# A perceiver layer on one core: the fourth piece of the scan moved around chunk 0's first products, the squares' tiles moved, and VectorE's first chunk reordered

## What is computed

```python
x = x + xattn(layernorm(x), ctx_1024, ...)     # attention over 257 context rows
h = layernorm(x)
xg = h * sigmoid(h @ Wg.T + bg)                # the gated tokens
# a linear scan over the 32 tokens, for each channel with its own 16x16 matrix A:
s = s @ A + xt * Bp;  y = (s * Cp).sum() + Dp * xt
y = y + xg
x = x + layernorm(y) * gamma + beta
h = layernorm(x) @ ternary(w_fc).T + gate * (layernorm(x) @ v.T @ fast_b.T @ u.T)
r = maximum(h, 0)
x = x + (r * r) @ ternary(w_proj).T
```

## Time and profile before

| | |
|---|---|
| time, median of 3 runs | 505.27 us (503.5 to 507.44) |
| time of the profiled execution | 506.74 us |
| its span on the core | 504.9 us |
| mean granted clock of PE | 0.988 |
| busy: PE, DVE, ACT, POOL | 94%, 81%, 71%, 68% of the span |

### The profile page before, as it was taken

The page is one execution under the profiler, slowest core; times in us unless marked ns, Lnnn a source line. Parts: engine busy times, 40 slices in busy tenths (PEclk is TensorE's granted clock), DMA queues, the critical chain, the costliest instruction groups (busy, mean ns, idle before and its releaser), DMA issues.

```text
span 504.9 us, 13692 instructions
## 1 busy us (share of the span) xinstructions
PE 472.9 (94%) x4374; PEld 403.6 (80%) x4374; DVE 408.9 (81%) x1203; ACT 356.6 (71%) x881; POOL 341.3 (68%) x446
## 2 busy tenths in 40 slices
PE   3799999999999998999999899887999999999995
PEld 2488788788888887888878788675888888888885
DVE  1689988889998899899998977787778798798654
ACT  3767677787877877577778577654877876877752
POOL 1478988776766767567767567222878887887563
PEclk9999999999999999899999899998999999999999
DMA  7944377586655747357657458675103303301102
GB/s 220 309 168 143 131 225 187 158 239 154 212 160 158 215 133 230 119 153 189 194 138 218 138 115 206 129 221 172 30 1 84 86 0 84 85 1 43 43 0 84
DMA packets 77974, 70.40 MB, mean 139 GB/s; under 512 B 40000, under 2 KB 60752, under 8 KB 77392
## 3 DMA queue, kind: packets, MB, share of 16 engines
q1 hardware_dynamic: 77904, 69.54, 48.5%
HBM read 56.87 MB, written 12.65 MB: 138 GB/s over the span
## 4 chain that ended last, share of the span: by engine, by line
PE 58%; DVE 10%; issue 9%; POOL 6%; ACT 3%; SPq 2%; DMA 1%; POOLq 0%; DVEq 0%; ACTq 0%
PE qv_ps L810 16%; PE turn_ps L799 9%; PE att_ps L861 5%; PE gate_ps L889 5%; PE fc_ps L1705 5%; PE score_ps L874 4%; PE proj_ps L1726 4%; POOL sq_lo L1842 3%; PE gate_ps L881 2%; PE feat_ps L850 2%; DVE bn_x L356 1%; PE xt_ps L1697 1%; PE xt_ps L1688 1%; PE feat_ps L930 1%; DVE scan_x L1887 1%
## 5 line engine op out<-in xcount | busy, mean ns | idle before, releaser
L1842 POOL TENSOR_TENSOR sq_lo<-scan_x,sq_hi 128x512 fp32r<-128x512 f32 x63 | 82.9, 1318 | 34.4 <-ACT sq_hi L1797 34.2
L1025 ACT COPY ctxT<-turn_ps 128x512 f32<-128x512 f32 x128 | 68.9, 590 | 33.4 <-PE turn_ps L799 32.0
L1789 ACT ACTIVATE relu<-fc_ps,fc_square 128x512 f32<-128x512 f32 x64 | 43.8, 685 | 33.3 <-PE fc_ps L1711 33.2
L1887 DVE SCALAR_TENSOR_TENSOR scan_x<-fc_ps,relu 128x512 f32<-128x512 f32 x64 | 43.7, 685 | 26.4 <-ACT relu L1789 25.8
L1212 POOL TENSOR_TENSOR hb_lo<-hbT,hb_hi 128x256 fp32r<-128x256 f32 x32 | 25.4, 795 | 49.0 <-ACT hb_hi L1100 49.0
L1705 PE MATMUL fc_ps<-xn_hi,fc_T 128*128 128x512 f32 x128 | 52.1, 407 | 2.1 <-DVE scan_x L1887 2.1
L799 PE MATMUL turn_ps<-ident,ctxn 128*128 128x128 f32 x352 | 49.1, 286 | 3.9 <-ACT ctxT L1025 2.6
L1705 PE MATMUL fc_ps<-xn_lo,fc_T 128*128 128x512 f32 x128 | 50.7, 396 | 0.0
L1204 POOL TENSOR_TENSOR proj_in<-proj_in,below 128x512 f32<-128x512 f32 x31 | 48.1, 1550 | 2.0 <-DVE below L1380 1.8
L1198 POOL TENSOR_TENSOR rstd<-ve,neg_half 128x1 f32<-128x1 f32 x64 | 35.2, 549 | 20.5 <-DVE ve L1445 15.7
L799 PEld LDWEIGHTS turn_ps<-ident,ctxn 128*128 128x128 f32 x352 | 42.4, 148 | 4.8 <-ACT ctxT L1025 3.1
(11 more groups left out here) (250 smaller groups left out, 1455.2 us busy)
## 6 DMA issues: line engine op xcount, KB each, us to landing
ctxn<-in_ctx SPq DMA_DIRECT2D x22, 1024.0 KB, 5.5
toeplitz<-in_ctx SPq DMA_DIRECT2D x10, 1024.0 KB, 5.7
resid<-in_x SPq DMA_DIRECT2D x32, 128.0 KB, 5.5
ctx_end<-in_ctx SPq DMA_DIRECT2D x32, 128.0 KB
gated_tokens<-gated SPq DMA_DIRECT2D x32, 128.0 KB, 6.0
scan_x<-gated_tokens SPq DMA_DIRECT2D x60, 64.0 KB, 4.8
out<-resid SPq DMA_DIRECT2D x7, 512.0 KB, 3.3
scan_quarters<-scan_x SPq DMA_DIRECT2D x3, 1024.0 KB, 5.3
```

Source lines behind the costliest of these rows:

```text
L1025: act.copy(ctxT[:, b, :, 0:J - 1], turn_ps[b % 2][:, :].rearrange("p (k j) -> p k j", k=KD)).then_inc(ctxT_copied, 1)
L1789: act.activation(relu[m % 2], fc_ps[m % 2][:, :], ACT.Relu, scale=fc_square[:, m:m + 1]).then_inc(relu_done, 1)
L1842: pool.tensor_tensor(sq_lo[:, tile(c, m) % PARTS, :], sq[m % SQ], sq_hi[:, tile(c, m) % PARTS, :].bitcast(F32), ALU.subtract).then_inc(sq_ ...
L1887: dve.scalar_tensor_tensor(out=sq[m % SQ], in0=fc_ps[m % 2][:, :], scalar=0.0, in1=relu[m % 2], op0=ALU.max, op1=ALU.mult).then_inc(sq_don ...
```

## The change

Nothing is changed in stage one, on SP or on POOL. In stage three:

- Scan blocks 8 to 11 (third piece) use the banks `proj_ps[0]` and `fc_ps`; blocks 12 to 15 (fourth piece) alternate over the two banks `proj_ps[1]`. `xt_ps` is not used by the scan any more, and `turn_first` has no wait for scan copies.
- PE runs blocks 8 to 13, then `turn_first`, block 14, `low_rank(0)`, both wides and both lows of tiles 0 and 1, block 15, and goes on as before. ACT copies block 14 after the two `xn_hi`, and block 15 in the loop at m = 1, behind `relu_tile(0, 1)` and `square_hi(0, 0)`.
- `sq` lies in `fc_in`, the loaded fc weights, which are turned into `fc_T` by then.
- DVE: the helpers take one half. The order is centre half 0, x of half 0, centre half 1, normalise half 0, x of half 1, `xn_lo` half 0, normalise half 1, y sums of chunk 1 half 0, `xn_lo` half 1, y sums half 1. `second_centre` is split: half 0 where it was, half 1 behind the square of tile 0.

The diff, with the bodies that only moved into helpers of one half cut:

```diff
-            for h in range(2):
-                for r in half(h):
-                    ins = dve.scalar_tensor_tensor(out=y_in[:, r, :], in0=y_in[:, r, :], scalar=mv_y[:, r, 0:1],
...
+        def first_centre(dve, h):
...
+        def first_x(dve, h):
...
+        def first_norm(dve, h):
...
-        def second_centre(dve):
+        def second_centre(dve, h):
...
-            tiles = scan_x[:, :, :].rearrange("p (i t) q -> p i (t q)", i=BATCH * CQ // TOK)
-            sq = [tiles[:, (PIECES - 1) * PB * CQ // TOK + i, :] for i in range(SQ)]
-            assert SQ * TOK <= PB * CQ
+            tiles = fc_in[:, :, :].rearrange("p (i a) d -> p i (a d)", i=SQ)
+            sq = [tiles[:, i, :] for i in range(SQ)]
+            assert SQ * TOK == MT * D
...
-            last_ring = (*proj_ps[0], *fc_ps, *xt_ps)
+            third_banks, fourth_banks = (*proj_ps[0], *fc_ps), proj_ps[1]
+            FOURTH = (PIECES - 1) * BLOCKS
+
+            def scan_bank(n):
+                return third_banks[n % BLOCKS] if n < FOURTH else fourth_banks[n % 2]
+
...
-                    at_least(pe, scan_copied, n - len(last_ring) + 1 if n - len(last_ring) >= 2 * BLOCKS else 0)
-                    scan_products(pe, n, last_ring[n % len(last_ring)])
+                    if n == FOURTH:
+                        pe.wait_ge(w_copied, 11)
+                    at_least(pe, scan_copied, n - 1 if n >= FOURTH + 2 else 0)
+                    scan_products(pe, n, scan_bank(n))
...
                         pe.wait_ge(xn_done, h + 1)
-                        if h == 0:
-                            pe.wait_ge(scan_copied, PIECES * BLOCKS)
...
                     at_least(pe, sq_done, tile(c, m) - 1)
+                    if tile(c, m) < 2:
+                        pe.wait_ge(scan_copied, FOURTH - 1 + m)
...
                         at_least(pe, out_ready, 2 * (c - 1))
+                        if c == 1:
+                            pe.wait_ge(scan_copied, PIECES * BLOCKS)
...
-                for n in range(2 * BLOCKS, PIECES * BLOCKS):
+                for n in range(2 * BLOCKS, FOURTH + 2):
                     last_scan(n)
                 turn_first()
+                last_scan(FOURTH + 2)
                 low_rank(0)
...
                             for i in range(2):
                                 hidden_low(0, i)
+                            last_scan(FOURTH + 3)
...
-                for n in range(2 * BLOCKS, PIECES * BLOCKS):
-                    scan_copy(act, n, last_ring[n % len(last_ring)])
+                for n in range(2 * BLOCKS, FOURTH + 2):
+                    scan_copy(act, n, scan_bank(n))
...
                              ).then_inc(xn_hi_done, 1)
+                scan_copy(act, FOURTH + 2, scan_bank(FOURTH + 2))
                 low_rank_hi(0)
...
                             square_hi(c, m - 1)
+                        if c == 0 and m == 1:
+                            scan_copy(act, FOURTH + 3, scan_bank(FOURTH + 3))
...
-                first_y(dve)
-                first_x(dve)
-                y_sums(dve, 1, range(CH))
-                for h in range(2):
+                def first_lo(h):
...
+                first_y(dve)
+                first_centre(dve, 0)
+                first_x(dve, 0)
+                first_centre(dve, 1)
+                first_norm(dve, 0)
+                first_x(dve, 1)
+                first_lo(0)
+                first_norm(dve, 1)
+                y_sums(dve, 1, half(0))
+                first_lo(1)
+                y_sums(dve, 1, half(1))
                 y_moments(dve, 1)
                 low_rank_parts(0)
-                second_centre(dve)
+                second_centre(dve, 0)
...
                             if m == 0:
+                                second_centre(dve, 1)
                                 second_add(dve, 0)
```

More of the change, by code:

```diff
@@ L259, in first_y @@
                 dve.tensor_scalar(ve_y[:, rows_of(h)], mv_y[:, rows_of(h), 1], EPS, None, ALU.add).then_inc(ve_y_done, 1)
-            for h in range(2):
-                for r in half(h):
-                    ins = dve.scalar_tensor_tensor(out=y_in[:, r, :], in0=y_in[:, r, :], scalar=mv_y[:, r, 0:1],
-                                                   in1=gamma_all[:, :], op0=ALU.subtract, op1=ALU.mult)
-                ins.then_inc(centred, 1)
-        def first_x(dve):
-            for h in range(2):
[L269 to L290, removed]
@@ L292, in second_centre @@
-        def second_centre(dve):
-            dve.wait_ge(mv_y_done, whole_chunks(2))
[L295 to L299, removed]
+        def first_centre(dve, h):
+            for r in half(h):
+                ins = dve.scalar_tensor_tensor(out=y_in[:, r, :], in0=y_in[:, r, :], scalar=mv_y[:, r, 0:1],
+                                               in1=gamma_all[:, :], op0=ALU.subtract, op1=ALU.mult)
+            ins.then_inc(centred, 1)
@@ new lines, in first_x @@
+        def first_x(dve, h):
+            dve.wait_ge(centred, h + 1)
+            dve.wait_ge(rstd_y_done, h + 1)
+            for r in half(h):
+                ins = dve.scalar_tensor_tensor(out=res(0, r), in0=y_in[:, r, :], scalar=rstd_y[:, r:r + 1],
+                                               in1=res(0, r), op0=ALU.mult, op1=ALU.add)
+            ins.then_inc(x2_done, 1)
+            dve.wait_ge(x2_done, h + 1)
+            for r in half(h):
+                ins = dve.bn_stats(bn_x[:, r, :], res(0, r))
+            ins.then_inc(bn_x_done, 1)
+            dve.wait_ge(bn_x_done, h + 1)
+            for r in half(h):
+                ins = dve.bn_aggr(mv_x[:, r, :], bn_x[:, r, :])
+            ins.then_inc(mv_x_done, 1)
+            dve.wait_ge(mv_x_done, h + 1)
+            dve.tensor_scalar(ve_x[:, rows_of(h)], mv_x[:, rows_of(h), 1], EPS, None, ALU.add).then_inc(ve_x_done, 1)
@@ new lines, in first_norm @@
+        def first_norm(dve, h):
+            dve.wait_ge(rstd_x_done, h + 1)
+            for r in half(h):
+                ins = dve.tensor_scalar(xn[:, r, :], res(0, r), mv_x[:, r, 0:1], rstd_x[:, r:r + 1],
+                                        ALU.subtract, ALU.mult)
+            ins.then_inc(xn_done, 1)
+        def second_centre(dve, h):
+            dve.wait_ge(mv_y_done, whole_chunks(2))
+            for r in half(h):
+                ins = dve.scalar_tensor_tensor(out=y_second[:, r, :], in0=y_second[:, r, :], scalar=mv_y[:, r, 0:1],
+                                               in1=gamma_all[:, :], op0=ALU.subtract, op1=ALU.mult)
+            ins.then_inc(centred, 1)
```

## The result

The changed kernel took 512.68 us (median of 4, 510.99 to 515.4) against 506.36 us before (median of 4, 503.5 to 509.28); the ratio is 1.0135 with a 95% interval of 1.0087 to 1.0182: slower by 1.35%, or 6.8 us by the ratio (the two medians lie 6.3 us apart). The forecast was 511.3, range 508.0 to 514.0. Six more executions gave 511.82 against 505.71, ratio 1.0125 (1.0085 to 1.0165). All ratios here leave out four executions that ran in a slower state: two of e3's ten (1162 and 2550 us) and two of the kernel before (511.36 and 512.38 us).

What follows compares the result with a forecast made beforehand. PE was taken to bound the kernel, with chunk 2's delayed load coming onto its path at tile 3. 4.8 + 1.5 - 0.3 = +6.0 us on the median of 505.27 gave 511.3 us, range 508.0 to 514.0.

Steps and rivals of the forecast that it cites:

- The view: PE's waits at the head of stage three decide; what is late at tile 3 is late at the end, us for us.
- Steps 1 and 2: DVE's and PE's head: half 1 normalised 0.9 us later than before, `low_rank(0)` at 342.8 against 342.44.
- step 2: PE's head: half 0 turned at once, half 1 at 340.75 to 341.3, so `low_rank(0)` can start at 342.8.
- Step 3: PE's clock in the head: lows of tiles 0 and 1 0.3 us earlier, bounds -1.2 and +1.0.
- Step 4: Block 15 free in PE's gap, its copy done ten us later; `second_centre` half 1 adds 0.8 us on DVE, hidden.
- Step 5: Chunk 2's load behind the sixteenth copy: 4.5 us from issue to sums, wides of tile 3 +4.8 us.
- Step 6: PE's clock falls after idling before tile 3: slow matmuls cost 1.5 us, bounds 0 and 1.6.
- Step 7: Small waits of PE in chunk 0 are absorbed: -0.3 us, bounds -0.5 and 0.
- the other side: Rival: chunk 2's y is there when DVE asks, blocks 14 and 15 fill gaps, 1.2 us saved, 504.1 us; chance 0.06.
- the cheaper wait: Rival: clock stays up or recovers at once, or the head gains 1.2 us; 4.0 instead of 6.0, 509.3 us; chance 0.08.
- the worse head: Rival: block 14 at half clock delays `low_rank(0)` (+1.0), load takes 5.4 us (+0.9); 513.5 us; chance 0.06.

Runs made afterwards that it cites:

- e3: Changed kernel with the sums of chunk 2's half 0 behind the square of tile 1, load still late; ratio to the kernel before 1.0082.
- a2: The changed kernel measured again, unedited; ratio to the kernel before 1.0125, 182.39 us from the first sums to the end.
- e1: Changed kernel with chunk 2's y loaded ahead of SP's wait for the sixteenth scan copy; ratio to the kernel before 1.0054.
- e5: e1 with `second_centre` whole again, ahead of the square of tile 0; ratio to the kernel before 0.9976.
- e4: Changed kernel with the edits of e1 and e3 together; ratio to the kernel before 1.0061.
- e8: e5 with e3's edit, block 14 ahead of `turn_first` again and DVE's head reordered; ratio to the kernel before 0.9988.
- e6: Kernel before with the sums of chunk 2's half 0 behind the square of tile 1; ratio to the kernel before 0.9984.
- e7: Kernel before with only `second_centre` split, half 1 behind the square of tile 0; ratio to the kernel before 1.0063.
- e2: Kernel before with SP waiting for the high part of tile 0's square before loading chunk 2's y; ratio to the kernel before 1.0112.

## Why the prediction was right, and where it was off

- **The view** held: nothing outside the head of stage three counts, and what is late at tile 3 is late at the end.
- **Steps 1 and 2** (DVE's and PE's head): half 1 was normalised at 10.66 against a forecast of 10.6, and `low_rank(0)` at 13.25, the slow one of the two ends given; block 14 did run at half speed. "The first half is ahead, the second pays for it" is what the trace shows. (The terms of step 2 add up to 342.5 and not to its 342.7; no later step hangs on the difference.) Left open by a2 and the other runs is only which way the clock goes there: e1's `low_rank` stood at 13.65 and its lows at 16.56, e5's at 12.90 and 17.02; in e1 block 14 ran at half pace, in e3, e4 and e5 it did not and the slow matmuls came in `low_rank` instead.
- **Step 3**: the lows at 16.76, forecast 16.4.
- **Step 4**: the sixteenth copy at 19.75 against 19.5; block 15 and its copy cost nothing, as said (e8, e6). What step 4 had wrong is `second_centre` half 1: it was put at 0.8 us, hidden. It was hidden, but it costs 1.9 (e7), since it pushes `second_add` beside POOL. In the changed kernel that made no difference, as DVE was done at 347.99 and waited until 351.04.
- **Step 5**: 4.48 us from issue to sums, forecast 4.5 (a2 4.47, e2 4.09). Tile 3 is +5.00 us, forecast +4.8. This is the mechanism, shown from both sides: e1 takes it out and e2 puts it in.
- **Step 6 failed in size.** The slow matmuls behind the wait were put at 1.5 us, bounds 0 and 1.6, from the 3.4 us that the clock was low in the head of before. After 5.55 us of waiting the matmuls ran at half pace until about 358.4, that is 6.0 us. From the wides of tile 3 to the second projection's start (358.52) it took 6.08 us, before 3.38: 2.70 lost, 2.25 in e2, 1.54 in e7. The upper bound was taken from a single stretch, and it was no bound. The rows of before:

```profile
354.11 0.64 PE L1726 MATMUL proj_ps<-proj_T,sq_hi 128*128 128x256 f32 x4
...
357.69 1.09 PE L1688 MATMUL xt_ps<-ident,xn 128*128 128x128 f32 x8
```

- **Step 7** was about right: from 358.52 on, 3.42 us to chunk 1's turns against 3.58 before, so 0.16 of small waits was absorbed, and another 0.05 behind the turns; 0.2 in all, where 0.3 was forecast.

Sum: 5.00 + 2.70 - 0.21 = 7.49, where 4.8 + 1.5 - 0.3 = 6.0 was forecast. By time it was 6.8 us (1.0135 of 506.36, interval 4.4 to 9.2). The forecast of 511.3 was 1.4 below the median, inside the range; 1.1 of that is the kernel before, whose median of four is 506.36 where the forecast started from 505.27. The change itself thus looks nearly hit, 6.3 us between the medians against 6.0, and that is closer than the steps earned: by the traces the sum was 1.5 us short, 1.2 of it slow matmuls. The times are too coarse to tell 6.0 from 7.5. Of the rivals, the other side and the cheaper wait are refuted by the rows above. Of the worse head, block 14 did run at half clock and delay `low_rank(0)`, but the lows came as early as before and the load took 4.5 us, not 5.4.

## What to carry to other kernels

When a producer is moved to a later slot, look at everything that waits on its *count*, in every queue: here a load that needed blocks 4 to 7 stood behind a wait for block 15, and one line on SP turned a move that gains nothing and costs nothing into 7 us. A gap on PE of some microseconds can cost more than its length, because the clock can fall in it or shortly behind it: here another 2.7 us behind 5.55. And work of 0.8 us put ahead of a two-input operation on VectorE can cost 1.9, if the operation then lands beside a GpSimd operation that reads SBUF too.

## What the hardware showed that was not expected

- VectorE's `second_add` (two inputs and the output in SBUF, 128x256 f32) took 1492 ns instead of 476 when GpSimd's `square_lo` had been issued while the operation before it ran, and `square_lo` took 1.58 us instead of 1.28. In e1, `square_lo` ran from 346.90 to 348.48, and `second_add` ended at 348.77, 0.3 us behind it: it seems to have stood until GpSimd was done, and did not share. The profile shows this as busy time of VectorE, not as a wait: it is found by comparing one operation's time with its like. The squares, with one input in PSUM, took 0.68 to 0.69 us beside the same GpSimd operation (e6, e8), as they do alone. The Trainium skill says this ("SBUF — State Buffer", Who interferes with whom): a VectorE instruction with two SBUF inputs and a GpSimd instruction that reads SBUF exclude one another for their whole length, and one with at most one SBUF input is free, unless it runs in a mode that takes both ports. The runs agree, with 1.0 us for one collision.
- The clock's return is not one number: behind a wait of 2.41 us it cost 1.5 us in e7 and nothing in e1 (6.97 us from tile 3 to the turns, before 6.96). Nor does it have to fall in the gap: in e7 the granted clock fell at about 352.4, 1.3 us after PE had begun again at 351.14, and in e4 at about 352.1, behind a wait of only 1.77 us that ended at 351.74. What decides it, no run here isolates. One and the same head gave the lows at 15.26 to 15.28 (e6, e2) or 16.65 to 16.72 (e7, before). That is why a profile of one execution can look 1.4 us better or worse than its kernel.
